# A one-core decoder kernel whose last attention multiplies values by probabilities: values become the stationary side, in column groups of 32

## The reference

```python
gating = softmax(x @ W_gate.T)
indicator = one_hot(argmax(gating), 16); top1 = indicator * max(gating)
q, k, v = split(x @ W_qkv.T, 3)                      # each (8, 128, 256)
k_shared = einsum('bth,bthd->btd', indicator, k)     # (8, 128, 16)
v_shared = einsum('bth,bthd->btd', top1, v)          # (8, 128, 16)
att = softmax(causal(einsum('bhqd,bkd->bhqk', q, k_shared) / 4))
y = einsum('bhqk,bkd->bhqd', att, v_shared)          # back to (8, 128, 256)
out = layernorm(x + y)
```

## Time and profile before

| | us |
|---|---|
| median of three runs | 372.49 (372.28 to 373.48) |
| the profiled execution | 370.43 |
| its span | 368.5 |
| PE, DVE, ACT, POOL busy in the span | 325.6, 274.5, 226.3, 207.5 |

### The profile page before, as it was taken

The page is one execution under the profiler, slowest core; times in us unless marked ns, Lnnn a source line. Parts: engine busy times, 40 slices in busy tenths (PEclk is TensorE's granted clock), DMA queues, the critical chain, the costliest instruction groups (busy, mean ns, idle before and its releaser), DMA issues.

```text
span 368.5 us, 5868 instructions
## 1 busy us (share of the span) xinstructions
PE 325.6 (88%) x1912; PEld 257.9 (70%) x1912; DVE 274.5 (74%) x527; ACT 226.3 (61%) x703; POOL 207.5 (56%) x291
## 2 busy tenths in 40 slices
PE   1958899999999999999999999673889999999993
PEld 0745778788778788778788788552477767777783
DVE  2774966955966955966955956988889999998662
ACT  4548567666567666667666655322467687688772
POOL 0488654756754756753756752885948767822200
PEclk9989999999999999999999999997789999999996
DMA  7911000031010031000040000000000000000000
GB/s 258 343 54 57 4 28 2 1 116 57 1 30 0 3 114 59 1 28 2 0 126 0 2 2 0 3 0 0 0 4 0 16 14 1 18 16 14 0 16 28
DMA packets 5757, 13.05 MB, mean 35 GB/s; under 512 B 992, under 2 KB 3168, under 8 KB 5472
## 3 DMA queue, kind: packets, MB, share of 16 engines
q1 hardware_dynamic: 5184, 11.90, 9.5%
q10 hardware_dynamic: 544, 0.79, 0.7%
HBM read 11.63 MB, written 1.05 MB: 34 GB/s over the span
## 4 chain that ended last, share of the span: by engine, by line
PE 61%; DVE 25%; issue 8%; ACT 2%; POOL 2%; DMA 1%; POOLq 0%; DVEq 0%; ACTq 0%
PE bank L357 13%; PE bank L478 12%; PE bank L388 8%; PE bank L374 7%; PE bank L467 5%; PE bank L456 3%; DVE toep L1029 3%; PE bank L636 3%; DVE t_cos L1219 2%; DVE neg_max L1283 2%; DMA x_raw<-in_xt 1%; PE bank L625 1%; PE bank L584 1%; DVE t_cos L996 1%; DVE v_tok L1208 1%
## 5 line engine op out<-in xcount | busy, mean ns | idle before, releaser
L1431 POOL TENSOR_TENSOR prob<-prob,rden 128x512 f32<-128x512 f32 x32 | 33.5, 1047 | 72.3 <-DVE rden L1056 72.3
L1410 POOL TENSOR_TENSOR t_sin<-rot,sin 128x512 f32<-128x512 f32 x40 | 54.3, 1359 | 27.4 <-ACT rot L752 24.7
L776 ACT ACTIVATE prob<-bank,neg_max 128x128 f32<-128x128 f32 x128 | 45.4, 368 | 39.2 <-DVE neg_max L1049 39.1
L357 PE MATMUL bank<-x_hi,w_hi 128*128 128x512 f32 x96 | 37.2, 470 | 8.6 <-ACT w_hi L733 8.1
L912 ACT ACTIVATE prob<-bank,neg_max 128x128 f32<-128x128 f32 x128 | 36.8, 375 | 11.7 <-DVE neg_max L1283 11.3
L388 PEld LDWEIGHTS bank<-k_rope,q_rope 128*128 128x128 f32 x256 | 34.6, 198 | 10.3 <-DVE q_rope L1009 4.9
L478 PE MATMUL bank<-wo_hi,head_hi 128*128 128x256 f32 x128 | 39.0, 304 | 3.0 <-DVE head_lo L1083 3.0
L388 PE MATMUL bank<-k_rope,q_rope 128*128 128x128 f32 x256 | 35.1, 282 | 4.5 <-DVE q_rope L1009 4.5
L300 POOL TENSOR_TENSOR q_rope<-y,rot 128x128 f32<-128x128 f32 (+7 forms) x60 | 31.4, 530 | 10.2 <-ACT rot L862 10.2
L478 PE MATMUL bank<-wo_lo,head_hi 128*128 128x256 f32 x128 | 36.1, 282 | 0.0
L478 PE MATMUL bank<-wo_hi,head_lo 128*128 128x256 f32 x128 | 36.1, 282 | 0.0
(11 more groups left out here) (106 smaller groups left out, 813.5 us busy)
## 6 DMA issues: line engine op xcount, KB each, us to landing
w_raw<-in_wqkv SPq DMA_DIRECT2D x3, 768.0 KB, 4.9
toep<-in_toep SPq DMA_DIRECT2D x8, 256.0 KB, 3.2
wo_raw<-in_wo SPq DMA_DIRECT2D x4, 512.0 KB, 3.5
x_raw<-in_xt SPq DMA_DIRECT2D x2, 512.0 KB, 6.1
ctxT<-in_ctx SPq DMA_DIRECT2D x1, 1024.0 KB, 9.0
x<-in_x SPq DMA_DIRECT2D x1, 1024.0 KB, 10.2
out<-x SPq DMA_DIRECT2D x8, 128.0 KB, 1.7
wf<-in_wf SPq DMA_DIRECT2D x1, 784.0 KB, 4.6
```

The source lines that it names most:

```text
L357: last = pe.matmul(out[:, :], wp[:, c, col:col + P], xp[:, j, c, :], start=(c + n == 0), stop=(c == C - 1 and n == 2))
L776: last = act.activation(prob[:, k % 2, h * P:(h + 1) * P], score_bank[k % 2][:, h * P:(h + 1) * P], ACT.Exp, bias=neg_max[:, k % 2, h:h + ...
L1410: pool.tensor_tensor(t_sin[:, par, :].rearrange("p (b t) -> p b t", b=BH), rot[:, par, :].rearrange("p (b t) -> p b t", b=BH), sin[:, :].u ...
L1431: pool.tensor_tensor(own, own, rden[:, k % 2, :].unsqueeze(2).to_broadcast([P, HG, P]), ALU.mult).then_inc(norm_done, 1)
```

## The change

`fvalues` swaps its sides. The values, widened to 32 columns (16 values, the column of ones, 15 zeros), are now stationary, and the transposed probabilities of one head, 128 columns, are streamed. Head h of the chunk uses the column group that begins at column 32h, and its result lands on 32 partitions of `y_bank`, with tokens along the free side. After the fourth chunk a new step on ACT, `yT_copy(b)`, copies the whole bank (128 by 512) into `vT`, and a new step on PE, `y_turn(b)`, transposes it in four pieces into `kvf_bank`, from which `y_invert` and `y_scale` now read. The two uses of `kvf_bank` are kept apart by new waits in `kv_project` and `y_turn`. On DVE the y chain of batch b moves to the end of `seq(b)`, behind `second_apply(b + 3)` and `query_lo(b + 2)`, and `norm_apply(b)` moves from the end of `seq(b)` into `seq(b + 1)`, behind its first `frow_max`.

```diff
--- before.py
+++ after.py
@@ -39,6 +39,7 @@
 FB = P // FD
 FC = 4
 CW = FC * FD
+YW = 32
 EPS = 1e-5
 CONV = 4
 
@@ -140,7 +141,8 @@
         ksT = x_raw[:, 1, P:2 * P]
         ksT_hi = sb("ksT_hi", [P, P], FP32R)
         ksT_lo = sb("ksT_lo", [P, P], FP32R)
-        vext = sb("vext", [P, NB, FD + 1])
+        vext = sb("vext", [P, NB, YW])
+        yT = vT[:, :]
         yden = sb("yden", [P, FH])
         ynorm = x_raw[:, 1, 2 * P:4 * P].rearrange("p (h d) -> p h d", d=FD)
 
...
@@ -581,6 +585,7 @@
 
                 if c == 0:
                     at_least(pe, masked_done, b, 1)
+                    at_least(pe, ynorm_done, b, 3)
                 last = pe.matmul(kvf_bank[:, :], x2T[:, j, c * P:(c + 1) * P], wf[:, c, D:3 * D],
                                  start=(c == 0), stop=(c == C - 1))
                 if c == C - 1:
@@ -630,12 +635,22 @@
                 pe.wait_ge(fptcopy_done, 4 * b + c + 1)
                 if c == 0:
                     pe.wait_ge(vext_done, b + 1)
-                    at_least(pe, ynorm_done, b, 1)
+                    at_least(pe, yT_copied, b, 1)
                 for h in range(4):
-                    f = 4 * c + h
-                    last = pe.matmul(y_bank[:, f * (FD + 1):(f + 1) * (FD + 1)],
-                                     probT[:, c % 2, h * P:(h + 1) * P], vext[:, b, :],
-                                     start=True, stop=True)
+                    last = pe.matmul(y_bank[h * YW:(h + 1) * YW, c * P:(c + 1) * P], vext[:, b, :],
+                                     probT[:, c % 2, h * P:(h + 1) * P], start=True, stop=True,
+                                     tile_position=(0, h * YW))
+                if c == FC - 1:
+                    last.then_inc(yT_done, 1)
+
+            def y_turn(b):
+
+                pe.wait_ge(yT_copied, b + 1)
+                pe.wait_ge(masked_done, min(b + 3, NB))
+                at_least(pe, ynorm_done, b, 1)
+                for c in range(FC):
+                    last = pe.transpose(kvf_bank[:, c * P:(c + 1) * P], yT[:, c * P:(c + 1) * P],
+                                        ident[:, :])
                 last.then_inc(y_done, 1)
 
             phase_a(pe, unit)
@@ -663,6 +678,8 @@
 
             def seq(b, j):
                 query_project(b + 1, 1 - j)
+                if b:
+                    y_turn(b - 1)
                 fturn(b, 1)
                 fscores(b, j, 3)
                 x2_turn(b + 2, j)
@@ -715,6 +733,7 @@
                 fvalues(b, 3)
 
             phase_b(pe, seq, last_seq)
+            y_turn(NB - 1)
 
         @block.scalar
         def _(act):
@@ -918,6 +937,11 @@
                 act.wait_ge(fpt_done, 4 * b + c + 1)
                 act.copy(probT[:, c % 2, :], fprobT_bank[c % 2][:, :]).then_inc(fptcopy_done, 1)
 
+            def yT_copy(b):
+                act.wait_ge(yT_done, b + 1)
+                at_least(act, y_done, b, 1)
+                act.copy(yT, y_bank[:, :]).then_inc(yT_copied, 1)
+
             phase_a(act, unit)
 
 
@@ -955,6 +979,7 @@
                 fprob_copy(b, 3)
                 fexps(b + 1, 1)
                 key_copy(b + 2)
+                yT_copy(b)
                 fprob_copy(b + 1, 0)
                 block_keys_hi(b + 2, j)
 
@@ -1010,6 +1036,7 @@
                                   ).then_inc(rope_done, 1)
 
             dve.memset(half_pow[:, :], -0.5)
+            dve.memset(vext[:, :, FD + 1:YW], 0.0)
             dve.memset(vext[:, :, FD:FD + 1], 1.0).then_inc(const_set, 1)
 
             def split_lo(lo, raw, hi, hi_ready, count, done):
@@ -1284,13 +1311,13 @@
                                   fscore_bank[c % 2][:, :].rearrange("p (h k) -> p h k", h=4),
                                   axis=AX.X, op=ALU.max, negate=True).then_inc(fmax_done, 1)
 
-            y = y_bank[:, 0:FH * (FD + 1)].rearrange("p (h d) -> p h d", h=FH)
+            y = kvf_bank[:, :].rearrange("p (h d) -> p h d", h=FH)
 
             y_flat = ynorm[:, :, :].rearrange("p h d -> p (h d)")
 
             def y_invert(b):
 
-                dve.wait_ge(y_done, 4 * b + 4)
+                dve.wait_ge(y_done, b + 1)
                 dve.reciprocal(yden[:, :], y[:, :, FD]).then_inc(yden_done, 1)
 
             def y_scale(b):
@@ -1330,6 +1357,8 @@
             def seq(b, j):
                 first_apply(b + 4, j)
                 frow_max(b, 3)
+                if b:
+                    norm_apply(1, ln3, b - 1, y_flat, x[:, b - 1, :])
                 mix_sum(b + 3, 1 - j)
                 frow_max(b + 1, 0)
                 gating(b + 2)
@@ -1337,22 +1366,21 @@
                 frow_max(b + 1, 1)
                 add_mix(b + 3, 1 - j)
                 norm_stats(0, ln2, b + 3, x1[:, 1 - j, :])
+                norm_aggr(0, ln2, b + 3)
+                norm_eps(0, ln2, b + 3)
+                frow_max(b + 1, 2)
+                second_apply(b + 3, 1 - j)
+                query_lo(b + 2, j)
                 y_invert(b)
-                norm_aggr(0, ln2, b + 3)
                 y_scale(b)
-                norm_eps(0, ln2, b + 3)
                 add_ffn(b)
                 norm_stats(1, ln3, b, y_flat)
-                frow_max(b + 1, 2)
                 norm_aggr(1, ln3, b)
-                second_apply(b + 3, 1 - j)
                 norm_eps(1, ln3, b)
-                query_lo(b + 2, j)
-                norm_apply(1, ln3, b, y_flat, x[:, b, :])
 
             def last_seq(b, j):
                 frow_max(b, 3)
-                if b > NB - 4:
+                if b:
                     norm_apply(1, ln3, b - 1, y_flat, x[:, b - 1, :])
                 if b + 1 < NB:
                     frow_max(b + 1, 0)
@@ -1369,20 +1397,18 @@
                     norm_stats(0, ln2, b + 3, x1[:, 1 - j, :])
                 if b + 1 < NB:
                     frow_max(b + 1, 2)
-                y_invert(b)
                 if b + 3 < NB:
                     norm_aggr(0, ln2, b + 3)
+                    norm_eps(0, ln2, b + 3)
+                    second_apply(b + 3, 1 - j)
+                if b + 2 < NB:
+                    query_lo(b + 2, j)
+                y_invert(b)
                 y_scale(b)
-                if b + 3 < NB:
-                    norm_eps(0, ln2, b + 3)
                 add_ffn(b)
                 norm_stats(1, ln3, b, y_flat)
                 norm_aggr(1, ln3, b)
-                if b + 3 < NB:
-                    second_apply(b + 3, 1 - j)
                 norm_eps(1, ln3, b)
-                if b + 2 < NB:
-                    query_lo(b + 2, j)
 
             phase_b(dve, seq, last_seq)
             norm_apply(1, ln3, NB - 1, y_flat, x[:, NB - 1, :])
```

More of the change, by code:

```diff
@@ L239, in decoder_kernel @@
         fptcopy_done = sem("fptcopy_done")
+        yT_done = sem("yT_done")
+        yT_copied = sem("yT_copied")
         y_done = sem("y_done")
```

## The result

The changed kernel takes 385.34 us in the median (384.09 to 387.32), against 372.38 for the kernel before: 1.0353 times as long, with a 95% interval of 1.0299 to 1.0408. The forecast was 386.0. Its profiled execution took 385.65 us, with a span of 383.5. That is 15.2 us more than the profiled execution of before, somewhat more than the medians differ (13.0): the profiled execution of before, 370.43, lay 1.95 us under its median, that of the changed kernel 0.31 us above.

A forecast was written before the change was run, and what follows sets the result against it. DVE paces batches 0 to 3, mostly PE from batch 5. Terms 8.8, 1.85, 1.4, 0.6 and 0.9 sum to 13.55 us on the profiled 370.43: 384.0; 2.06 more for a median gives 386.0, range 379.5 to 391.

The forecast's parts named there:

- Steps 1 to 3: Early batches: ACT's copy delays query_lo 0.26 us, DVE waits there, the y chain behind it delays first_apply 1.98 us.
- the ring: Batches 0 to 3: DVE's frow_max releases ACT's run, which releases query_lo, then the next frow_max; +8.8 us in all.
- Step 4: Growth in batches 0 to 3: 2.33 us a batch, 1.98 in batch 0; sum 8.8 us at frow_max(4, 3).
- The signs: Expected in the trace: DVE waits 1.5 to 2 us at query_lo; first_apply to first_apply 15.2 to 15.7 us.
- The forecast's own bounds: Whole kernel: chunk cost, smaller growth from DVE and POOL contention (2.9 us off), or longer hops give 381 to 390.5 us.
- Rival (c): PE's clock falls from about 2 us idle a batch: 412 us, or 392 to 399 for a batch or two; chance 0.05.
- Step 5: PE's fvalues chunk of eight matmuls: 0.5 us assumed, between 0.25 and 1.0, against 0.81 before.
- Steps 6 to 9: Batches 4, 5, 6 and 7: +1.85, +1.4, +0.6 and +0.9 us from the copy, turn and later y chain.
- the tail: Batch 7, last fprob_copy to y_invert: copy and turn add 1.3 us, last chunks may return 0.4; +0.9.
- Rival (a): PE's matmul saving sets the pace from batch 4 on: -4.7 us, so 367.8; chance 0.04.
- The lower bound: Low end of the forecast's bounds for the whole kernel's time, given as 381 us.

The follow-up runs named there:

- experiment 3: Changed kernel with the y chain placed ahead of query_lo on DVE instead of behind it; 376.80 us, ratio 1.0149 to the kernel before.
- experiment 5: Whole changed computation with fvalues(b, 3), y_turn and yT_copy in other places and DVE's order of before; 370.63 us, ratio 0.9929 to the kernel before.
- experiment 6: Changed kernel with ACT copying the bank a second time, into an unused buffer, ahead of yT_copy; 390.18 us.
- experiment 4: Changed kernel with 14 small filler matmuls on PE ahead of x1_turn in batches 0 to 3; 382.37 us, ratio 1.031 to the kernel before.
- experiment 2: Kernel before with only the swapped matmuls in column groups, no copy or turn, DVE's old order, output not right; 367.94 us, ratio 0.991.
- experiment 8: New-places kernel (experiment 5) with batch 7 multiplying as before, without copy or turn; 369.23 us, ratio 0.9891 to the kernel before.
- experiment 1: Kernel before with only DVE's order of the changed kernel, old matmuls, no copy or turn; 388.72 us profiled, 398 to 400 in the other three runs.

## Why the prediction was right, and where it was not

The time was right (386.0 forecast, 385.34 measured), and so was the mechanism. That the two agree to 0.7 us is luck. The sum holds errors of opposite sign, and the forecast added 2.06 us to come from a profiled execution to a median. Between the profiled executions 13.55 us were forecast and 15.2 measured; the changed kernel's profiled execution lay 0.31 us above its median, where the forecast put it 2.06 under.

- **Steps 1 to 3, the ring.** The places are right: the copy moved `query_hi`, the chain took 1.98 us behind `query_lo`, and DVE waited 1.90 us there in batches 0 to 3 (1.5 to 2 were forecast, in batches 0 to 5; batch 4 has 0.66 and batch 5 has 2.14). PE idled 1.49 us for `x1_turn` (about 2). Experiments 3, 5 and 6 move, hide or double one part of it, and the time follows.
- **Step 4, the ring's growth.** Mis-sized: 2.33 us a batch forecast, 1.78 measured (experiment 4). The signs had 15.2 to 15.7 us a batch; with the clock up it is 14.95, and with it down 15.83 and 17.00. Of the missing 0.55 us, 0.45 lie between `first_apply` and `frow_max(b+1, 1)`: 7.22 us before, so 7.57 by the forecast, and 7.12 measured. `norm_apply` did come in there, but `gscore` took 0.29 us less and the step from `first_apply` to the next `frow_max` 0.12 less. The first two rows are `gscore` and the POOL product beside it in the kernel before, the third is the product beside `gscore` in experiment 4 (307.23 us in its rows above):

```profile
303.36 0.61 DVE L1240 SCALAR_TENSOR_TENSOR gscore<-gate,gneg,ties 128x16 f32<-128x16 f32 x1
303.29 0.66 POOL L303 TENSOR_TENSOR q_rope<-y,rot 128x192 f32<-128x192 f32 x1
306.87 0.65 POOL L307 TENSOR_TENSOR q_rope<-y,rot 128x192 f32<-128x192 f32 x1
```

  Both times `gscore` ended 0.02 or 0.03 us after the product that was running when it began; before, that product had 0.59 us left, in experiment 4 it had 0.29. The forecast's own bounds had room for it ("should contention between DVE and POOL fall otherwise"). In the profiled pair, with the waits for `kv_project` taken out (1.05, 2.11 and 2.15 us in batches 1 to 3), batches 0 to 3 grew by 6.2 us, and in experiment 4 by 7.3, not 8.8.
- **Rival (c), the clock.** It was given 0.05 and, in a mild form, it happened: those waits, 5.3 us in the profiled run. The argument against it, that 2 us of idle time come in pieces, did not hold: 1.49 and 0.63 us in front of `x1_turn` were enough. By experiment 4 it is less: 4.2 us in the traces, 3.0 in the medians, 1.6 by the ratios. The forecast's sum had no term for it.
- **Step 5, the chunk.** 0.5 us assumed, 0.35 and 0.09 measured. The Trainium skill ("TensorEngine Tiling (Array Packing)", Key Properties) lets tiles run in parallel and makes a change of mode drain the engine. The trace agrees with the first. `kv_project`, whose operands are of the chunk's type (fp32), takes 1.80 us for four instructions of 512 streamed columns (its start to the next row's, 302.12 to 303.92 in the kernel before), so the chunk's eight of 128 would take 0.90 one after the other, an estimate, and they take 0.35. What part the narrower loads have in it, 32 columns in place of 128, no run separates. The 0.09 us ahead of a chunk may be the drain; no run separates that either.
- **Steps 6 to 9, the late batches.** Forecast +1.85, +1.4, +0.6 and +0.9; measured +1.70, +1.26, +0.71 and +0.11. Only the tail is off. Before, its last two chunks had run at a falling clock (2.52 us for 16 instructions, granted clock 0.74 in 360 to 364 us); in the changed kernel a chunk's row has 0.43, and the granted clock is 1.00 from 372 to 380 us. In experiment 4, where it fell in the tail (0.51 in 372 to 376 us), the same stretch grew by 0.79. So the 0.9 fits a tail at a fallen clock, and which it will be the forecast could not tell.
- **Rival (a)**, PE's saving, has a true core: experiment 2 gains 3.1 us with nothing but the matmuls. It decides once the new steps stand where no one waits for them (experiments 5 and 8).
- **The lower bound** of 381 is a slip: 386.0 - 1 - 2.9 is 382.1. Nothing hangs on it.

So: -0.3 us up to the beginning of the stage, +6.2 ring, +5.3 clock, +3.8 late batches, 15.0 between the spans of the profiled pair, where the forecast had 8.8 + 4.75 and no clock.

## What to carry to other kernels

Before work is moved in a hand-written order, look for the step at which two engines meet with little time to spare (here 0.26 us), and follow the ring through it: an engine that is busy 60% of the span can be in it. Work that must be added goes ahead of the wait, in the shadow of the other engine, and not behind it; the same copies and turns made the kernel 3.5% slower in one place and 0.7% faster in another. And an engine that is not the bound can still become it: its idle time can cost it its clock. What of that idle time does so, no run here settles.

## What was unexpected of the hardware

- Idle stretches of 0.63 and 1.49 us on PE with one `fturn` between them were followed by some 7 us at 1.2 GHz (clock 0.64 and 0.51 in two windows of 4 us), and in experiment 1 a single one of 1.51 us was too. But 0.63 and 0.48 us in the same place left the clock at 2.4 GHz (experiment 3), so did 14 small matmuls in the gap (experiment 4), and so did 0.63 and 1.51 us in batch 4 of the changed kernel, with 2 us of matmuls between them. The length of a gap alone doesn't tell.
- The same small DVE operation (`gscore`, 128x16) took 0.23 to 0.63 us. In the traces of all ten kernels it ended 0.01 to 0.03 us after the POOL product that was running when it began, if that had more than 0.23 us left, and otherwise took 0.23 or 0.24: 0.63 at 316.54 in the kernel before, where the product had 0.61 left, and 0.23 at 329.89, when POOL was idle.
- The order alone made runs of one kernel on one chip differ by 11 us (388.7 to 399.9), with mean granted clocks of 0.94 and 0.91; those of experiment 2, in which no gap on PE in batches 0 to 3 is longer than 0.85 us, stayed within 1.3 (367.0 to 368.3).
